# Token choice layer: expert outputs regrouped by block transposes on the vector engine instead of through memory

## The reference

```
grouped = x.reshape(x.shape[:-2] + (-1, ne, d))            # groups of ne = 16 tokens
logits = jnp.einsum('...btd,des->...btes', grouped, controller)
perm = (logits + tie == max over the 16 tokens).astype(x.dtype)
sel = jnp.einsum('...btd,...btes->...besd', grouped, perm)
inner = relu(jnp.einsum('...besd,desf->...besf', sel, f1) + bias)
inter = jnp.einsum('...besf,esfd->...besd', inner, f2)
out = jnp.einsum('...besd,...btes->...btd', inter, perm)
```

## Time and profile before

| | us |
|---|---|
| median of 3 runs | 2503.06 (2500.81 to 2505.09) |
| the profiled execution, its own time | 2499.96 |
| span of that execution in the trace | 2498.1 |
| TensorE busy | 2175.6 (87%) |
| DVE busy | 1420.4 (57%) |
| ACT busy | 996.3 (40%) |
| POOL busy | 901.0 (36%) |

### The profile page before, as it was taken

How to read it: one execution, slowest core, us unless ns; L and a number is a source line. 1 busy time by engine, 2 the same in 40 slices (tenths; PEclk the granted TensorE clock), 3 DMA queues, 4 the chain that set the end, 5 groups by cost and what they waited for, 6 DMA issues and landing times.

```text
span 2498.1 us, 42625 instructions
## 1 busy us (share of the span) xinstructions
PE 2175.6 (87%) x17140; PEld 1362.6 (55%) x17140; DVE 1420.4 (57%) x2526; ACT 996.3 (40%) x1450; POOL 901.0 (36%) x573
## 2 busy tenths in 40 slices
PE   4899999999999999888878699999688888888885
PEld 2445555555555555566656556775455555555553
DVE  3545555555555555546566435544467777677772
ACT  1233333333333333444535243334245554555443
POOL 4222222222222220203123022101448877787784
PEclk7899999999999999999999899999789999999997
DMA  6555555555555554376796832101654465445511
GB/s 146 124 109 116 116 112 111 111 111 111 111 111 111 111 103 69 129 245 236 267 306 219 288 123 68 49 19 51 181 140 116 109 179 137 139 111 155 130 35 51
DMA packets 228355, 328.81 MB, mean 132 GB/s; under 512 B 14928, under 2 KB 167488, under 8 KB 227904
## 3 DMA queue, kind: packets, MB, share of 16 engines
q1 hardware_dynamic: 221168, 321.49, 49.2%
q10 hardware_dynamic: 6992, 4.60, 0.7%
HBM read 197.46 MB, written 127.93 MB: 130 GB/s over the span
## 4 chain that ended last, share of the span: by engine, by line
PE 57%; DVE 17%; DMA 7%; POOL 6%; ACT 6%; issue 3%; SPq 3%; ACTq 1%; DVEq 0%; POOLq 0%
PE l0a_slot L775 8%; PE l0a_slot L785 7%; PE l0a_O L710 6%; DVE l1f_rowmax L1978 5%; PE l1a_slot L1570 4%; PE l0a_slot L752 4%; POOL l1f_added L1855 3%; DMA l0f_wide<-expert_outputs 2%; PE l0a_slot L757 2%; ACT l0f_f L590 2%; PE l1a_slot L1561 2%; DMA expert_outputs<-l0f_wide 2%; PE l0a_slot L803 2%; DVE l0f_hidden L655 2%; PE l1a_slot L1612 2%
## 5 line engine op out<-in xcount | busy, mean ns | idle before, releaser
L590 ACT ACTIVATE l0f_f<-l0a_slot 128x1024 f32<-128x1024 f32 (+1 forms) x256 | 248.6, 972 | 339.0 <-PE l0a_slot L775 189.2
L655 DVE TENSOR_REDUCE l0f_hidden<-l0a_slot 128x4 f32<-128x1024 f32 (+1 forms) x256 | 293.5, 1156 | 114.2 <-PE l0a_slot L785 111.2
L1927 ACT ACTIVATE l1f_probs<-l1f_slot 128x1024 f32<-128x1024 f32 x240 | 244.1, 1023 | 251.0 <-PE l1f_slot L2109 245.7
L1978 DVE TENSOR_REDUCE l1f_rowmax<-l1f_slot 128x1 f32<-128x1024 f32 x240 | 287.5, 1217 | 70.1 <-PE l1f_slot L2100 69.7
L1855 POOL TENSOR_TENSOR l1f_added<-l1f_probs 128x1024 f32<-128x1024 f32 x117 | 277.4, 2371 | 133.1 <-ACT l1f_probs L1927 125.3
L775 PE MATMUL l0a_slot<-l0f_hidden 128*128 128x512 bf16 (+1 forms) x1024 | 296.0, 374 | 13.5 <-DMA l0f_hl<-qk_rows 9.1
L549 POOL TENSOR_TENSOR l0f_x<-l0f_x 128x512 f32<-128x512 f32 x32 | 40.8, 1274 | 538.6 <-DVE l0f_x L639 538.6
L2109 PE MATMUL l1f_slot<-l1f_Qs,l1f_Ks 128*128 128x256 f32 x960 | 171.5, 302 | 37.7 <-DVE l1f_lo L1968 14.8
L2100 PE MATMUL l1f_slot<-l1f_Ks,l1f_Qs 96*128 96x512 f32 x480 | 173.7, 447 | 26.0 <-DVE l1f_rowmax L1978 19.9
L2109 PEld LDWEIGHTS l1f_slot<-l1f_Qs,l1f_Ks 128*128 128x128 f32 x960 | 144.1, 194 | 93.1 <-DVE l1f_rowmax L1978 29.8
L710 PE MATMUL l0a_O<-l0f_f,l0f_wide 128*32 128x128 f32 x3840 | 156.1, 279 | 9.4 <-issue 9.4
(11 more groups left out here) (194 smaller groups left out, 3750.3 us busy)
## 6 DMA issues: line engine op xcount, KB each, us to landing
expert_outputs<-l0f_wide SPq DMA_DIRECT2D x64, 512.0 KB, 5.3
l0f_wide<-expert_outputs SPq DMA_DIRECT2D x32, 1024.0 KB, 11.5
l1f_Ks<-kq_rows SPq DMA_DIRECT2D x48, 512.0 KB, 8.7
l0a_Qs<-qk_rows SPq DMA_DIRECT2D x90, 256.0 KB, 7.9
l0f_hl<-qk_rows SPq DMA_DIRECT2D x90, 256.0 KB, 14.9
qk_rows<-l0f_wide SPq DMA_DIRECT2D x32, 512.0 KB, 2.8
qk_rows<-l0f_x SPq DMA_DIRECT2D x32, 512.0 KB, 4.1
l0f_f<-in_dram SPq DMA_DIRECT2D x32, 512.0 KB, 7.7
```

Source lines behind the costliest of these rows:

```text
L590: exp_ready.by(act.activation(probs[:, t % 2, HG * g:HG * g + HG, 0:reach, :], s[:, :, 0:reach, :], ACT.Exp, scale=SCALE))
L655: max_ready.by(dve.reduce_max(rowmax[:, t, :, 2 * g:2 * g + 2], s[:, :, :, first:2 * P], AX))
L1927: exp_done.by(act.activation(probs[:, half, u - FIRST[b], :], s[:, :], ACT.Exp, scale=SCALE))
L1978: max_done.by(dve.reduce_max(rowmax[:, i:i + 1], s[:, :], AX))
```

## The change

The scratch in DRAM, its 64 stores and its 32 gather DMAs go. ACT copies the whole slot of an `inter` step, 1024 words, and DVE no longer takes part in it. When all 8 copies of a half are there, DVE transposes `wide` in place: 8 instructions (`turn`), each of 32 x 32 words per partition, in which a 32 by 32 block lies between 32 partitions and 32 experts. The word that is read next, and the one that is written next, lies 256 words (1 KB) behind the last. So that the groups lie in the order that 32 by 32 blocks give, `sel` is written in another order of groups, in runs of 4 words where there were runs of 16. The `turn` steps are spread among the selection of the next half, and `out` waits for all eight.

```
-    steps = [(-1, "gather", 1), (0, "f2", 2), (0, "f2", 3)] + s[2:] + e[:1] + late + [(-1, "aggregate", 0), (0, "spread", 1)]
+    def turns(offset, half):
+        return [(offset, "turn", NTURN * half + n) for n in range(NTURN)]
+
+    steps = [(0, "f2", 2), (0, "f2", 3)] + merged(s[2:], turns(-1, 1)) + e[:1] + late + [(-1, "aggregate", 0), (0, "spread", 1)]
...
-    steps += [(-1, "store", 1), (-1, "store", 0), (0, "gather", 0), (1, "load", 0), (1, "load", 1), (0, "f2", 6), (0, "f2", 7)]
+    steps += [(-1, "store", 1), (-1, "store", 0), (1, "load", 0), (1, "load", 1), (0, "f2", 6), (0, "f2", 7)]
     s, e, early = selection(1), experts(1), combination(0, 0)
-    steps += s[2:] + e[:1] + early + [(1, "xT", n) for n in range(4)] + [(1, "logits", 0), (1, "second", 0)]
+    steps += merged(s[2:], turns(0, 0)) + e[:1] + early + [(1, "xT", n) for n in range(4)] + [(1, "logits", 0), (1, "second", 0)]
...
+        by_quad = sel[:, :, :, :].rearrange("p c e (j q) -> p c e j q", j=J)
+        by_word = wide[:, :, :].rearrange("p e d -> p d e")
...
-                if kind == "inter":
-                    half, n = divmod(i, IN)
-                    inter_even.wait(sp, X, i + 1)
-                    alone(sp)
-                    inter_odd.wait(sp, X, i + 1)
-                    left[half].by(sp.dma_start(scratch[half, :, 4 * n:4 * n + 4, :], wide[:, 4 * n:4 * n + 4, :]))
...
-                if kind == "gather":
-                    wait_alone(sp, left[i].sem, (X + 3) * IN * 16)
-                    rows = scratch[i, :, :, :].rearrange("(q j) e d -> (j e) q d", j=J)
-                    for n in range(NC):
-                        q = slice(NQ // NC * n, NQ // NC * (n + 1))
-                        back[n].by(sp.dma_start(wide[:, q, :], rows[:, q, :]))
...
-                    s = arrived(act, X, step)[:, 0:512].rearrange("p (g e) -> p e g", e=EH)
+                    s = arrived(act, X, step)[:, 0:512].rearrange("p (q j e) -> p e j q", q=4, j=J)
...
-                    sel_even.by(act.copy(sel[:, 0, :, 16 * tp:16 * tp + 16], s))
+                    sel_even.by(act.copy(by_quad[:, 0, :, :, 4 * tp:4 * tp + 4], s))
...
-                    inter_even.by(act.copy(wide[:, e:e + 4:2, :], s[:, 0:512].rearrange("p (e d) -> p e d", e=2)))
+                    outputs.by(act.copy(wide[:, e:e + 4, :].rearrange("p (n k) d -> p k n d", k=2), s[:, :].rearrange("p (k n d) -> p k n d", k=2, n=2)))
...
-                    sel_odd.by(dve.tensor_copy(sel[:, 1, :, 16 * tp:16 * tp + 16], s))
+                    sel_odd.by(dve.tensor_copy(by_quad[:, 1, :, :, 4 * tp:4 * tp + 4], s))
...
-                if kind == "inter":
-                    s = arrived(dve, X, step)
-                    e = 4 * (i % IN)
-                    inter_odd.by(dve.tensor_copy(wide[:, e + 1:e + 4:2, :], s[:, 512:1024].rearrange("p (e d) -> p e d", e=2)))
+                if kind == "turn":
+                    half, n = divmod(i, NTURN)
+                    if n == 0:
+                        outputs.wait(dve, X, IN * half + IN)
+                    part = by_word[:, D // NTURN * n:D // NTURN * (n + 1), :]
+                    turned_round.by(dve.transpose(part, part))
...
-                    back[i % NC].wait(pe, X, i // NC + 1)
+                    turned_round.wait(pe, X, NTURN * (i // NC + 1))
```

More of the change, by code:

```diff
@@ L817, in window_attention_layer, with token_choice_layer @@
                     spent=[(signal.sem, signal.step, signal.count(NBLOCK - 1)) for signal in spent])
-def token_choice_layer(nc, block, semaphores, kept, x_in, y_out, controller, f1_in, f2_in, f1_bias, tie_in, ident_in, scratch):
+def token_choice_layer(nc, block, semaphores, kept, x_in, y_out, controller, f1_in, f2_in, f1_bias, tie_in, ident_in):
     G = 16
@@ L838, in token_choice_layer @@
     NB = NSEQ // 2
+    NTURN = 8
     def selection(half):
@@ L901, in token_choice_layer @@
     hidden_even = signal("hidden_even", 2 * PAIRS); hidden_odd = signal("hidden_odd", 2 * PAIRS)
-    inter_even = signal("inter_even", 2 * IN); inter_odd = signal("inter_odd", 2 * IN)
-    left = [signal(f"left{half}", IN, 16) for half in range(2)]
+    outputs = signal("outputs", 2 * IN)
+    turned_round = signal("turned_round", 2 * NTURN)
     normed = [signal(f"normed{n}", NT) for n in range(2)]
-    back = [signal(f"back{i}", 2, 16) for i in range(NC)]
     summed = signal("summed", 2 * NC)
@@ L912, in reader @@
                 "h": [(hidden_even, HB * (i + 1)), (hidden_odd, HB * (i + 1))],
-                "inter": [(inter_even, i + 1), (inter_odd, i + 1)], "out": [(summed, i + 1)]}[kind]
+                "inter": [(outputs, i + 1)], "out": [(summed, i + 1)]}[kind]
     schedule.signals(filled, reader)
@@ L990, in start_sp @@
         def start_sp(self, sp):
-            for s in (*f2_loaded, *x_loaded, *stored, *left, *back):
+            for s in (*f2_loaded, *x_loaded, *stored):
                 s.start(sp)
@@ L998, in start_act @@
         def start_act(self, act):
-            for s in (hi_ready, xT_even, spread_ready[0], chosen_ready, sel_even, hidden_even, inter_even):
+            for s in (hi_ready, xT_even, spread_ready[0], chosen_ready, sel_even, hidden_even, outputs):
                 s.start(act)
         def start_dve(self, dve):
-            for s in (xT_odd, rated, best_ready, choice_ready, lo_ready[0], normed[1], sel_odd, hidden_odd, inter_odd, summed):
+            for s in (xT_odd, rated, best_ready, choice_ready, lo_ready[0], normed[1], sel_odd, hidden_odd, turned_round, summed):
                 s.start(dve)
@@ L1184, in piece @@
                     tp = i % TP
-                    s = arrived(dve, X, step)[:, 512:1024].rearrange("p (g e) -> p e g", e=EH)
+                    s = arrived(dve, X, step)[:, 512:1024].rearrange("p (q j e) -> p e j q", q=4, j=J)
                     if tp == 0:
                         schedule.wait_filled(dve, X if i else X - 1, ("h", 1 if i else 3))
-                    sel_odd.by(dve.tensor_copy(sel[:, 1, :, 16 * tp:16 * tp + 16], s))
+                    sel_odd.by(dve.tensor_copy(by_quad[:, 1, :, :, 4 * tp:4 * tp + 4], s))
                 if kind == "h":
@@ L1290, in programs @@
         return Tail([(s.sem, s.count(NB - 1)) for s in stored], [(s.sem, s.count(0)) for s in stored],
-                    [(b.sem, b.count(NB - 1)) for b in back], schedule.left())
+                    [(turned_round.sem, turned_round.count(NB - 1))], schedule.left())
     return First(), programs
@@ L2137, in four_layers @@
             with ExitStack() as kept:
-                first, programs = token_choice_layer(nc, block, semaphores, kept, x1, x2, controller, f1, f2, f1_bias, tie, ident,
-                                                     dram("expert_outputs", (2, 128, 32, D)))
+                first, programs = token_choice_layer(nc, block, semaphores, kept, x1, x2, controller, f1, f2, f1_bias, tie, ident)
                 tail = window_attention_layer(nc, block, semaphores, x, x1, wq, wk, bq, bk, wv, bv, wo, bo, cos, sin, mask, maskT, ident,
```

## The result

The changed kernel takes 2562.55 us (median of 4 runs, 2556.97 to 2563.22), the kernel before 2501.93 us (4 runs, 2498.90 to 2505.09): a ratio of 1.0237, with a 95% interval of 1.0218 to 1.0257. It is slower by some 60 us. The profiled execution took 2563.22 us, 63.3 more than the one before. The forecast was 2561.

The account below looks back on a forecast made before the run. Memory-trip waits before `out` bound the changing layer; DVE's turns would then hold up h. Terms +21.6 +17.7 +12.2 -2.4 +0 +9.1 = +58.2 us on 2499.96 gave 2558.2, or 2561 on the median's scale; range 2525 to 2597.

Parts of the forecast that it names:

- Step 1, DMAs: Ahead of and within `out`: gather waits go, -4.7 us, and x's transposes wait less, -1.1 us, per second half.
- Step 2, ACT's copies: ACT's wider `inter` copies add 3 us per second half, 2.2 in block 0's first, 1.0 in the last.
- step 5: Three first halves: first turn 30.4 us after h, 3.5 us earlier than the last copy now; selection +9.4; +17.7 in all.
- Step 3, the turn: In the selection: a turn takes 2.05 us (bounds 1.76 to 2.29), making last copy to h 20.3 us.
- Steps 4 to 6: Halves of the layer: second halves +21.6 us, first halves +17.7, block 0's first half +12.2, the last half -2.4.
- Step 7, into the next layer: After the last copy: eight turns in a row take 15.9 us, but the way to the next layer changes by about 0.
- Step 8, the clock: TensorE's clock falls after idling ahead of h: 1.3 us for each of 7 selections, +9.1 us.
- The turn at the dense rate: Rival in the selection: a turn costs 1.22 us, hops cost nothing, kernel 2499 us; chance 0.16.
- The shut-out by POOL: Rival: turns wait for POOL's rescale in three selections, +30 us, kernel 2591 us; chance 0.10.
- Only the reads cost: Rival: only a turn's reads pay for hops, 1.76 us a turn, kernel 2542 us; within the forecast's spread, no separate chance.

Follow-up runs that it names:

- e4: The changed kernel without any turns, `out` waiting for ACT's copies and `wide` not regrouped: 2446.89 us, ratio 0.9783 to the kernel before.
- e5: The kernel before, memory trip kept, with ACT copying all 1024 words of an `inter` slot and DVE none: 2498.16 us, ratio 0.9996.
- e2: The changed kernel with turns that read `wide` with the 1 KB hop but write side by side into `hidden`: 2548.37 us, one run.
- e3: The changed kernel with turns that read side by side from `hidden` but write `wide` with the 1 KB hop: 2545.21 us, one run.
- e1: The changed kernel with each turn taking 1024 words side by side in `wide`, groups not regrouped: 2492.69 us, ratio 0.9967 to the kernel before.
- e9: The changed kernel with `wide` laid out in pairs, two experts' words side by side: 2500.03 us, ratio 0.9996 to the kernel before.
- e11: The changed kernel with all eight turns of a half behind the last `sel` copy: 2566.19 us, ratio 1.0262 to the kernel before.
- e10: The changed kernel with `wide` in pairs and four of each half's eight turns behind the last `sel` copy: 2470.48 us, ratio 0.9876 to the kernel before.
- e8: The changed kernel, slow turns included, with ACT copying both halves of each `sel` slot and DVE none: 2492.25 us, ratio 0.9976 to the kernel before.
- e7: The changed kernel with `wide` laid out experts innermost, so `out` streams words 128 bytes apart: 2537.88 us, ratio 1.0159 to the kernel before.

## Why the prediction was right, point by point

**The sum** was +58.2 and came out as +63.3 in the profiled execution, 2562.55 against 2561.0 in the medians. That it came so close is luck: e4 splits the sum into two, and both parts were too small. Without turns the steps gave -8.4 - 10.5 + 2.2 - 2.4 - 15.9 = -35.0; measured were -53.8. The turns gave 68.2 + 15.9 + 9.1 = 93.2; measured were 115.7. The errors of 19 and 22 us nearly cancelled. By pieces, profiled executions of the kernel before and e4 differ by -13.8 us in the second halves, -17.3 in the first and -23.6 from the last h to the next layer, where the steps gave -8.4, -10.5 and -18.3. The turns (changed kernel against e4) added 94.6 us up to the last h, clock included, for 77.3, and 19.8 behind it for 15.9.

**Step 1, DMAs.** Right that the waits go: no wait for a gather is left, and the steps of `out` follow in one run. Next to e5, which keeps the trip, e4's second halves are 6.8 to 9.2 us shorter, more than the 5.8 of step 1, and its last half with the way to the next layer is 23.6 us shorter than before (62.1 to 38.5), where the steps gave 18.3.

**Step 2, ACT's copies.** Its +3.0 was right in size (e5: +1.5 to +5.1 a second half). What failed is the sentence that DVE's 64 copies "are worth nothing by themselves": in a first half they stood between rescales and on TensorE's path. Their removal, with an aggregation that starts 2 us earlier after h (17.3 for 19.3), gives e5's -5.4 to -5.8, where step 5 took only 3.5 off. Part of the earlier aggregation is a shorter wait for a gather (1.28 us in place of 2.79 ahead of the second `out` step), so not all of it is owed to the copies.

**Step 3, the turn.** 2.05 us forecast, 2.22 measured, inside the bounds of 1.76 and 2.29, nearer the upper one and next to the 2.19 that the prediction worked out from the figure of the Trainium skill. The assumption under the middle value, that reading and writing overlap in part, holds (e2, e3: 720 + 710 give 1002), but the penalty of one side was 0.70 ns a word and not L623's 0.52. At 6.4 us for each 0.1 us this is 11 us at most, and in the selections it is 1 us each: 21.3 us from the last copy (1152.94 to 1153.95) to h at 1175.26, for 20.3.

**Steps 4 to 6.** The shape was right: h moves to the end of DVE's work. In the no-turn kernel the first turn's place in a first half, 30.4 us after h by step 5, is where its first `sel` copy ends (30.2 to 30.3). From the first `sel` copy to h it is 22.2 us against e4's 10.7 in the second halves and 22.0 against 9.8 in the first, so 11.5 and 12.2 us more, where 10.0 and 9.4 were forecast. That is the mis-sized term of the selections, besides the clock.

**Step 7, into the next layer.** Eight turns in a row took 16.44 us, for 15.9. The way came out 3.2 us shorter and not the same: 31.3 from the last copy, not 33.4.

```profile
1480.70 16.44 DVE L1195 STREAM_TRANSPOSE l0f_wide<-l0f_wide 128x1024 f32<-128x1024 f32 x8 [5.97 <-ACT l0f_wide L1159]
```

**Step 8, the clock.** The direction was right and the size too small. The seven h behind a selection with turns take 5.18 to 6.58 us, 2.1 more than 3.71 in the mean, where 1.3 was taken over from `out` steps. The matmuls of `sel` after TensorE's wait ran at half clock too, but there DVE sets the pace and it costs nothing more. One more place was not in the forecast: in the last of the three first halves the `inter` steps behind a wait of 2.64 us for POOL's spread copy took 2.08 us each in place of 1.14, which with the longer h (6.58 against 5.36) makes this half 4.2 us longer than the one before it.

**The rivals.** The turn at the dense rate fell for this layout, and e1 and e9 give what it would have cost: 2492.7 and 2500.0, around the 2499 worked out for it. The 311 ns that the prediction took for this rival from the Trainium skill (VectorE: DVE Perf Modes, The three transpose paths) are given there for bf16; no run here has a turn of bf16. The shut-out by POOL did not come: none of the 64 turns took more than 2355 ns, and beside POOL's rescale, 6.04 us from 1204.81 on, they keep their pace:

```profile
1204.81 6.04 POOL L936 TENSOR_SCALAR l0f_x<-l0f_x,l0f_ln_mv,l0f_ln_rstd 128x256 f32<-128x256 f32 x5
...
1206.95 2.35 DVE L1195 STREAM_TRANSPOSE l0f_wide<-l0f_wide 128x1024 f32<-128x1024 f32 x1
...
1209.79 4.29 DVE L1195 STREAM_TRANSPOSE l0f_wide<-l0f_wide 128x1024 f32<-128x1024 f32 x2
```

"Only the reads cost" fell with e3.

## What to carry to other kernels

Before an engine is given work in the shadow of others, add up all that it has to do between the two points, and compare this with what the path does there: here 21.4 us against 14. The one other order tried with such turns did not help (e11), while with light turns a new order gave 30 us (e10); moving the copies to ACT helped even with the slow turns (e8). The cost of this rearrangement within SBUF lay in single-word hops, and a layout with two words side by side served the vector engine and ACT in full and TensorE but for 5%; one that spares a single engine can charge the next (e7). And a sum that comes out right still deserves the run that splits it.

## What the runs showed of the hardware that was not expected

- DVE's penalty for single-word hops is the same for reads and writes (720 and 710 ns for 1024 words) and 1002 ns for both; with runs of 2 words and hops of 2 KB there is none (1224 ns against 1222 dense).
- TensorE streams float32 words 8 bytes apart at nearly the dense rate (64 matmuls of 256 columns in 7.43 us at full clock, 7.09 in the changed kernel, whose words are adjacent), and 128 bytes apart at less than half of it (15.7 us). The Trainium skill (SBUF — State Buffer, Door 1: The DMA port swizzle) says that consecutive accesses reach full bandwidth with at least two hits in a line of 16 bytes. e7 agrees with it, and e9 but for the 5%.
- An ACT copy of 1024 words from PSUM takes 1016 ns whether it writes rows (e1, e4), runs of 4 words 128 bytes apart (e7) or pairs (e9), though in e7 and e9 it also reads PSUM word by word, 1 or 2 KB apart.
